# Keys' squares of a sixteen-head attention folded in half on GpSimd before VectorE sums them

## The chip, the cores and the metric

The kernel runs on one core of a Trainium2 chip. The metric is the time of one execution on the device in microseconds, the median of the runs shown. Engines are called by their names here, and in the profile's rows PE is TensorE (PEld its weight loads), DVE is VectorE, ACT is ScalarE, POOL is GpSimd and SP is SyncE.

## What is computed

A state-space block with conditioning, then six layers of local attention and a gated feed-forward net, over 128 sequences of 32 tokens and 128 channels. The change is in the attention: queries and keys of each of 16 heads (64 elements each) are divided by their norms. Since a window is 32 tokens long and a sequence too, each sequence attends to itself alone.

```python
def l2norm(t):
    return t / jnp.maximum(jnp.linalg.norm(t, axis=-1, keepdims=True), 1e-12)
...
qkv = x @ Wqkv
q, k, v = jnp.split(qkv, 3, -1)
...
q = l2norm(q) * qs
k = l2norm(k) * ksc
...
q = q * cos * scale + rotate_half(q) * sin * scale
k = k * cos * inv + rotate_half(k) * sin * inv
out = local_attention(q, k, v)      # softmax(8 q k^T, masked) v
...
for i in range(DEPTH):              # 6 layers
    x = attn_layer(shift_tokens(x), ...) + x
    x = ffn_layer(shift_tokens(x), ...) + x
```

## The kernel before

The first part (`cond_block`) is the state-space block; the second (`stack`) is the six layers, and the change is there. The 4096 tokens are 32 tiles of 128 tokens (four sequences each); four tiles are a group, so a layer has 8 groups and the six layers have 48 groups and 192 tiles. The residual stream stays in SBUF.

Every engine runs its own hand-written list, `body(i, l, g)`: for each group the same steps in the same order, with a loop over the tiles j = 0 to 3 inside. The work is pipelined over tiles by the order of those lists: a step written with `back` works on the tile (or group) that many places earlier. While the projections of tile n run, the scores of tile n - 2 are scaled and exponentiated and the values of tile n - 3 are weighed. Engines wait for each other with semaphores that count tiles. In each layer the first two groups are written out, and the other six are a hardware loop. Two more bodies at the end drain the pipeline.

For tile n the norm work goes like this. TensorE projects the queries into a PSUM tile `pa` (L843). ScalarE squares them into `sq`, an area of SBUF of 128 x 1024 floats (`square_q`, L1041). VectorE sums each head's 64 squares (`sum_squares`, L1278, called with c = 0) into `ss`, and multiplies the queries by the cosine table (L1285) and the sine table (L1294). The same area `sq` then takes the squares of the keys (`square_k`, L1048), which wait for `sum_q`; `sq_k` tells that they are there. VectorE multiplies the keys by sine and cosine and then sums their squares (`sum_squares` with c = 1), which sets `sum_k`. ScalarE turns the sums into inverse norms `inv` (L1065, L1072, L1080). The next `square_q` waits for `sum_k`, since it writes over `sq`.

GpSimd's list for a tile, before: `norm_scores` of tile n - 2 (L1470, `sm` times the queries' inverse norm, after VectorE has subtracted the maximum, L1316), `rotate` of the queries and of the keys of tile n (L1454 twice), `norm_probs` of tile n - 2 (L1492, after `rden`), `norm_keys` of tile n (L1463). Every second tile it also makes the rounding remainder `xs_lo` (L1440), in tile 2 of a group the remainder of a piece of the next layer's weights (L1485), and in the second group of a layer those of `wo` (L1479, 128 x 1024) and `w1` (L1475, 128 x 682) and the next rotary tables.

VectorE's list for a tile, before: maximum of the scores (L1309), `turn_probs` of tile n - 3 (L1303, writes `prT` after `norm_probs`), sum of the queries' squares, queries times cosine and sine, `subtract_maximum` (L1316), keys times sine and cosine, sum of the keys' squares, denominators (L1323) and their reciprocals, `oT_lo` (L1354). In tile 0 it also has the normalisation (L1342) and `fn_lo` (L1348, `fx` minus `fn_hi`, all three in SBUF) of an earlier group's feed-forward net; TensorE needs `fn_lo` for that net's first gate block (L960), which stands in its list in tile 1. In tile 3 it adds the attention to the residual (L1364).

TensorE's `project_v` of tile n waits for `sin_q` and `cos_q` of that tile, because it writes the PSUM tile that the queries leave. Its transposes (L872) wait for `oT_lo` of an earlier tile or for `norm_k`.

## Time and profile before

| | |
|---|---|
| median of 3 runs | 2878.83 us |
| lowest, highest | 2873.51, 2882.35 us |
| span of the profiled execution | 2876.3 us |
| mean granted TensorE clock | 0.988 of full speed |
| second part, from the first `fn_lo` to the last | 503.1 to 2856.6 us |
| busy: TensorE matmul, weight loads | 2709.0, 2060.1 us |
| busy: VectorE, ScalarE, GpSimd | 2616.4, 2273.1, 2115.9 us |

The rows below are from this one profiled execution. A busy share is an average over the whole span. A row of a timeline gives the start from the beginning of the span, then how long the instruction is recorded; consecutive instructions of an engine overlap by some hundredths of a microsecond in the record. What stands in brackets at a row's end is how long the engine sat idle before the instruction and which instruction's end released it. A row that groups instructions gives their number, the time that they are busy in total, the mean of one in nanoseconds, and the idle time ahead of them.

### The profile page before, as it was taken

The page shows a single profiled execution, that of the slowest core. Times are in us where ns is not written, and L with a number is a line of the kernel's source. Part 1 is how long each engine was busy: PE and PEld are TensorE (multiplying, and loading weights), DVE is VectorE, ACT ScalarE, POOL GpSimd, SP SyncE. Part 2 cuts the span into 40 slices and gives each one's busy share as a digit, 9 for nine tenths or more (in the row PEclk, how much of TensorE's full clock was granted, in tenths as well). Part 3 has the DMA queues.
Part 4 walks back from the last instruction along what each step waited for, and adds up shares of the span by engine and source line. Part 5 has one row for each costly group of instructions (what it writes and reads, how often), then busy time and mean ns, then how long its engine had stood idle before and what let it go on. Part 6 is the DMA issues. An engine that isn't in the chain of part 4 may idle for free.

```text
span 2876.3 us, 92923 instructions
## 1 busy us (share of the span) xinstructions
PE 2709.0 (94%) x36417; PEld 2060.1 (72%) x36417; DVE 2616.4 (91%) x3375; ACT 2273.1 (79%) x3824; POOL 2115.9 (74%) x1529
## 2 busy tenths in 40 slices
PE   8799978999999999999999999999999999999996
PEld 7577756777777777777777777777777777777774
DVE  6899968999999999999999999999999999999993
ACT  5799857878787887878788887878888787877873
POOL 5766658777778777777777787777777777877771
PEclk9899999999999999999999999999999999999998
DMA  1000013222223232232232233222322322322222
GB/s 57 23 2 2 1 36 76 70 71 65 71 63 76 71 76 64 66 78 67 67 76 68 66 74 73 69 67 68 75 68 66 78 65 63 72 67 58 63 66 78
DMA packets 103719, 178.41 MB, mean 62 GB/s; under 512 B 29350, under 2 KB 52708, under 8 KB 103396
## 3 DMA queue, kind: packets, MB, share of 16 engines
q1 hardware_dynamic: 102372, 174.60, 25.0%
q8 instruction: 124, 2.03, 0.3%
q10 hardware_dynamic: 1152, 1.20, 0.1%
q14 instruction: 71, 0.58, 0.1%
HBM read 22.62 MB, written 2.10 MB: 9 GB/s over the span
## 4 chain that ended last, share of the span: by engine, by line
POOL 26%; issue 24%; DVE 15%; PE 11%; ACT 5%; DMA 2%; POOLq 0%; DVEq 0%; SPq 0%; ACTq 0%
POOL spare L1454 15%; DVE spare L1285 5%; POOL pr L1492 4%; DVE qk_t L1294 3%; POOL spare L1463 3%; PE pa L843 3%; DVE ss L1278 3%; PE px L872 3%; DMA kT<-spare 2%; POOL xs_lo L1440 2%; DVE oT_lo L1354 1%; PE pg L982 1%; PE pg L930 1%; PE px L917 1%; POOL w_lo L1485 1%
## 5 line engine op out<-in xcount | busy, mean ns | idle before, releaser
L1454 POOL TENSOR_TENSOR spare<-spare,qk_t 128x1024 f32<-128x1024 f32 x384 | 910.2, 2393 | 11.5 <-POOL xs_lo L1440 8.1
L843 PE MATMUL pa<-w_hi,xs_hi 128*128 128x512 f32 x1152 | 511.8, 444 | 27.5 <-issue 8.4
L1470 POOL TENSOR_TENSOR sm<-sm,inv 128x512 f32<-128x512 f32 x192 | 201.8, 1051 | 446.7 <-DVE sm L1316 372.7
L1294 DVE TENSOR_TENSOR qk_t<-pa,rot 128x1024 f32<-128x1024 f32 x384 | 464.4, 1210 | 1.9 <-ACT spare L1048 1.7
L1285 DVE TENSOR_TENSOR spare<-pa,rot 128x1024 f32<-128x1024 f32 x384 | 464.5, 1210 | 0.0
L1278 DVE TENSOR_REDUCE ss<-spare 128x16 f32<-128x1024 f32 x384 | 457.5, 1191 | 6.7 <-ACT spare L1041 5.9
L843 PE MATMUL pa<-w_hi,xs_lo 128*128 128x512 f32 x1152 | 456.7, 396 | 0.0
L843 PE MATMUL pa<-w_lo,xs_hi 128*128 128x512 f32 x1152 | 454.9, 395 | 0.0
L872 PE MATMUL px<-ident_sb,spare 128*128 128x128 f32 x3072 | 409.0, 276 | 22.3 <-POOL spare L1463 11.6
L1463 POOL TENSOR_TENSOR spare<-spare,inv 128x1024 f32<-128x1024 f32 x192 | 365.9, 1906 | 80.6 <-ACT inv L1080 75.7
L872 PEld LDWEIGHTS px<-ident_sb,spare 128*128 128x128 f32 x3072 | 341.6, 141 | 111.0 <-issue 59.0
L843 PEld LDWEIGHTS pa<-w_hi,xs_hi 128*128 128x128 f32 x1152 | 217.9, 189 | 120.9 <-DVE qk_t L1294 45.5
L1354 DVE TENSOR_TENSOR oT_lo<-px,oT_hi 128x1024 fp32r<-128x1024 f32 x192 | 226.5, 1180 | 83.3 <-ACT oT_hi L1118 83.3
L903 PEld LDWEIGHTS ps<-kT,qT 128*32 128x32 f32 x12288 | 181.8, 110 | 128.7 <-issue 64.7
L903 PE MATMUL ps<-kT,qT 128*32 128x64 f32 x12288 | 212.2, 221 | 56.0 <-DMA kT<-spare 55.9
L1095 ACT COPY spare<-px 128x1024 f32<-128x1024 f32 x192 | 194.6, 1013 | 87.9 <-PE px L872 87.6
L1048 ACT ACTIVATE spare<-pa 128x1024 f32<-128x1024 f32 x192 | 196.5, 1024 | 77.3 <-DVE ss L1278 59.7
L843 PEld LDWEIGHTS pa<-w_hi,xs_lo 128*128 128x128 f32 x1152 | 217.7, 189 | 53.6 <-issue 0.5
L843 PEld LDWEIGHTS pa<-w_lo,xs_hi 128*128 128x128 f32 x1152 | 218.9, 190 | 49.1 <-issue 12.3
L1118 ACT CAST oT_hi<-px 128x1024 fp32r<-128x1024 f32 x192 | 193.4, 1007 | 69.5 <-PE px L917 68.1
L917 PEld LDWEIGHTS px<-pT,spare 64*64 64x64 f32 x12288 | 198.9, 136 | 68.9 <-issue 66.0
L241 PE MATMUL c_bank<-c_h,c_cdiag 64*64 64x256 f32 x2048 | 230.3, 380 | 10.4 <-DVE c_h L548 9.1
(180 smaller groups left out, 5970.0 us busy)
## 6 DMA issues: line engine op xcount, KB each, us to landing
kT<-spare SPq DMA_DIRECT2D x384, 256.0 KB, 3.7
pT<-prT SPq DMA_DIRECT2D x768, 64.0 KB, 2.0
w_part<-in_Wqkv SPq DMA_DIRECT2D x40, 192.0 KB, 3.7
wo<-in_Wo SPq DMA_DIRECT2D x6, 512.0 KB, 5.4
c_h<-in_x SPq DMA_DIRECT2D x4, 512.0 KB, 9.0
spare<-in_x SPq DMA_DIRECT2D x8, 256.0 KB, 5.0
out<-spare SPq DMA_DIRECT2D x8, 256.0 KB, 2.5
wo<-in_W SPq DMA_DIRECT2D x6, 341.0 KB, 5.2
```

The source lines that it names most:

```text
L241: last = pe.matmul(py[t % 2][rows, 0:DI], cdiag[rows, t % 3, n, :], h[rows, t % 2, n, :], start=False, stop=(n == DS - 1), skip_group_chec ...
L843: last = pe.matmul(pa[(u + c) % 2][:, half * 512:half * 512 + 512], x[:, j * P:(j + 1) * P], w[:, at], start=(k == 0), stop=(k == 2))
L872: last = pe.transpose(px[:, hp * P:(hp + 1) * P], qk_r[:, c, hp * P:(hp + 1) * P], ident[:])
L903: last = pe.matmul(ps[rows, hp * 2 * S:(hp + 1) * 2 * S], qT[:, hp, rows], kT[:, :, hp, b, :], start=False, stop=True, skip_group_check=True)
L917: last = pe.matmul(px[at:at + DH, to:to + 64], v[rows, j, h * DH:(h + 1) * DH], pT[rows, :, h, :], start=True, stop=True, skip_group_check ...
L1278: dve.reduce_sum(ss[:, c, :], heads(sq), AX.X).then_inc(s[sum_sem], 1)
L1285: dve.tensor_tensor(heads(qk_r[:, c, :]), heads(pa[(3 * j + c) % 2][:]), per_head(rot[:, l % 2, 2 * c, :]), ALU.mult).then_inc(s[cos], 1)
L1294: dve.tensor_tensor(halves(qk_t[:, c, :]), halves(pa[(3 * j + c) % 2][:])[:, :, ::-1, :], table.unsqueeze(1).to_broadcast([P, HEADS, 2, DH ...
L1354: dve.tensor_tensor(oT_lo[:, :, k, :].rearrange("p h (r q) -> p r h q", r=2), px[:].rearrange("p (r h q) -> p r h q", r=2, h=HP), oT_hi[:, ...
L1454: pool.tensor_tensor(qk_r[:, c, :], qk_r[:, c, :], qk_t[:, c, :], ALU.add)\
L1463: pool.tensor_tensor(k_r, k_r, over(inv[:, j % 2, 1, :], DH), ALU.mult).then_inc(s["norm_k"], 1)
L1470: pool.tensor_tensor(keys(sm[:]), keys(sm[:]), over(inv[:, j % 2, 0, :], S), ALU.mult)\
```

## The change

The sum of the keys' squares is made in two steps. GpSimd first adds, for each head, the upper 32 of the 64 squares to the lower 32, in place in `sq` (`fold_squares_k`), and signals `folded_k`. VectorE then sums the lower 32 of each head alone, behind `folded_k` in place of `sq_k`. The queries' squares are summed as before. The fold is the first step of GpSimd's list for every tile.

```diff
--- before.py
+++ after.py
@@ -664,7 +664,7 @@
 
         names = """const_loaded mask_ready zeroed xs_zeroed w_part_loaded w0_hi w0_ready wo_loaded kT_ready ffn_loaded
             qk_scale_loaded rot_ready w_hi_ready w_lo_ready xs_hi_ready xs_ready q_full k_full v_full
-            sq_q sq_k sum_q sum_k floored ln_done inv_ready
+            sq_q sq_k sum_q folded_k sum_k floored ln_done inv_ready
             cos_q cos_k sin_q sin_k rot_q rot_k norm_k tq_done tq_out tk_done tk_out v_out
             masked scores_done top_done sub_done scaled exp_done den_done rden_done probs_done turned pT_loaded pv_done pv_out oT_lo_ready wo_hi_ready wo_lo_ready
             wo_done res_attn fs_ready center_done fc_ready fsq_ready var_done fln_done frs_ready fn_mul fn_ready fn_hi_ready fn_lo_ready w1_loaded w1_hi_ready w1_lo_ready
@@ -1270,12 +1270,19 @@
 
             @block.vector
             def _(dve):
-                def sum_squares(i, j, back, c, sq_sem, sum_sem):
-                    n, j, live = tile(i, j, back)
-                    if live:
-                        dve.wait_ge(s[sq_sem], n + 1)
+                def sum_squares_q(i, j, back):
+                    n, j, live = tile(i, j, back)
+                    if live:
+                        dve.wait_ge(s["sq_q"], n + 1)
                         wait_for(dve, s["floored"], n)
-                        dve.reduce_sum(ss[:, c, :], heads(sq), AX.X).then_inc(s[sum_sem], 1)
+                        dve.reduce_sum(ss[:, 0, :], heads(sq), AX.X).then_inc(s["sum_q"], 1)
+
+                def sum_squares_k(i, j, back):
+                    n, j, live = tile(i, j, back)
+                    if live:
+                        dve.wait_ge(s["folded_k"], n + 1)
+                        wait_for(dve, s["floored"], n)
+                        dve.reduce_sum(ss[:, 1, :], heads(sq)[:, :, 0:DH // 2], AX.X).then_inc(s["sum_k"], 1)
 
                 def times_cos(i, j, l, c, sq_sem, transposed, cos):
                     n, j, live = tile(i, j, 0)
@@ -1388,7 +1395,7 @@
                             add_ffn(i, 2)
                         maximum(i, j, 2)
                         turn_probs(i, j, 3)
-                        sum_squares(i, j, 0, 0, "sq_q", "sum_q")
+                        sum_squares_q(i, j, 0)
                         if j == 2:
                             gated(i, 2, 2)
                         times_cos(i, j, l, 0, "sq_q", "tq_done", "cos_q")
@@ -1396,7 +1403,7 @@
                         subtract_maximum(i, j, 2)
                         times_sin(i, j, l, 1, "sq_k", "rot_k", "sin_k")
                         times_cos(i, j, l, 1, "sq_k", "tk_done", "cos_k")
-                        sum_squares(i, j, 0, 1, "sq_k", "sum_k")
+                        sum_squares_k(i, j, 0)
                         if j == 3:
                             add_attention(i, 1)
                         if j == 0:
@@ -1454,6 +1461,13 @@
                         pool.tensor_tensor(qk_r[:, c, :], qk_r[:, c, :], qk_t[:, c, :], ALU.add)\
                             .then_inc(s[rotated], 1)
 
+                def fold_squares_k(i, j, back):
+                    n, j, live = tile(i, j, back)
+                    if live:
+                        pool.wait_ge(s["sq_k"], n + 1)
+                        low, high = heads(sq)[:, :, 0:DH // 2], heads(sq)[:, :, DH // 2:DH]
+                        pool.tensor_tensor(low, low, high, ALU.add).then_inc(s["folded_k"], 1)
+
                 def norm_keys(i, j, back):
                     n, j, live = tile(i, j, back)
                     if live:
@@ -1513,6 +1527,7 @@
 
                 def body(i, l, g):
                     for j in range(GT):
+                        fold_squares_k(i, j, 0)
                         norm_scores(i, j, 2)
                         if j == 3:
                             shift_lo(i, -1, 0)
```

GpSimd's list from the last step of tile 3 of a group to tile 0 of the next group (here the first and second group of layer 0). L1463 is `norm_keys`, L1470 `norm_scores`, L1454 `rotate` of queries and keys, L1492 `norm_probs`. Before:

```order
L1463 TENSOR_TENSOR spare<-spare,inv 128x1024 [waits inv_ready,rot_k]
L1470 TENSOR_TENSOR sm<-sm,inv 128x512 [waits inv_ready,sub_done]
L1454 TENSOR_TENSOR spare<-spare,qk_t 128x1024 [waits cos_q,sin_q]
L1454 TENSOR_TENSOR spare<-spare,qk_t 128x1024 [waits cos_k,sin_k]
L1492 TENSOR_TENSOR pr<-pr,rden 128x512 [waits rden_done]
L1463 TENSOR_TENSOR spare<-spare,inv 128x1024 [waits inv_ready,rot_k]
```

And now, the same piece of the list (the line numbers are those of the changed kernel; L1477 is `norm_keys`, L1469 the fold, L1484 `norm_scores`, L1461 `rotate`, L1506 `norm_probs`):

```order
L1477 TENSOR_TENSOR spare<-spare,inv 128x1024 [waits inv_ready,rot_k]
L1469 TENSOR_TENSOR spare<-spare 128x16x32 [waits sq_k]
L1484 TENSOR_TENSOR sm<-sm,inv 128x512 [waits inv_ready,sub_done]
L1461 TENSOR_TENSOR spare<-spare,qk_t 128x1024 [waits cos_q,sin_q]
L1461 TENSOR_TENSOR spare<-spare,qk_t 128x1024 [waits cos_k,sin_k]
L1506 TENSOR_TENSOR pr<-pr,rden 128x512 [waits rden_done]
L1477 TENSOR_TENSOR spare<-spare,inv 128x1024 [waits inv_ready,rot_k]
```

The fold stands between the keys' norms of one tile and the scaling of the scores in the next, with a wait on `sq_k`; all else keeps its order.

VectorE's list around the sum of the keys' squares, tile 3 of a group. L1316 is `subtract_maximum`, L1294 and L1285 are the keys times sine and cosine, L1278 is the sum, L1364 adds the attention. Before:

```order
L1316 TENSOR_TENSOR sm<-ps,top 128x512 [waits exp_done,top_done]
L1294 TENSOR_TENSOR qk_t<-pa,rot 128x1024 [waits rot_k,sq_k]
L1285 TENSOR_TENSOR spare<-pa,rot 128x1024 [waits tk_done,sq_k]
L1278 TENSOR_REDUCE ss<-spare 128x16 [waits floored,sq_k]
L1364 TENSOR_TENSOR res<-pg,res 128x512 [waits wo_done]
```

And now (L1323, L1301, L1292, L1285 and L1371 in the changed kernel):

```order
L1323 TENSOR_TENSOR sm<-ps,top 128x512 [waits exp_done,top_done]
L1301 TENSOR_TENSOR qk_t<-pa,rot 128x1024 [waits rot_k,sq_k]
L1292 TENSOR_TENSOR spare<-pa,rot 128x1024 [waits tk_done,sq_k]
L1285 TENSOR_REDUCE ss<-spare 128x16 [waits floored,folded_k]
L1371 TENSOR_TENSOR res<-pg,res 128x512 [waits wo_done]
```

Nothing moved on VectorE; the sum waits for `folded_k` where it waited for `sq_k`, and its input is half as long.

## Rows read from the trace of the kernel before

**Rows 1.** The page, busy time of each engine (share of the span, instructions).

```profile
PE 2709.0 (94%) x36417; PEld 2060.1 (72%) x36417; DVE 2616.4 (91%) x3375; ACT 2273.1 (79%) x3824; POOL 2115.9 (74%) x1529
```

**Rows 2.** Groups of instructions: busy us, mean ns | idle before (L1475: min/median/max ns).

```profile
L1454 POOL TENSOR_TENSOR spare<-spare,qk_t 128x1024 f32<-128x1024 f32 x384 | 910.2, 2393 | 11.5 <-POOL xs_lo L1440 8.1
L1470 POOL TENSOR_TENSOR sm<-sm,inv 128x512 f32<-128x512 f32 x192 | 201.8, 1051 | 446.7 <-DVE sm L1316 372.7
L1278 DVE TENSOR_REDUCE ss<-spare 128x16 f32<-128x1024 f32 x384 | 457.5, 1191 | 6.7 <-ACT spare L1041 5.9
...
L1323 DVE TENSOR_REDUCE den<-pr 128x16 f32<-128x512 f32 x32 | 21.6, 674 | 0.0
L1485 POOL TENSOR_TENSOR w_lo<-w_part,w_hi 128x384 f32 x6 | 6.1, 1018 | 0.0
...
L1475 POOL TENSOR_TENSOR w_lo<-wo,w_hi x6: 1682/1686/1689, 494.5 to 2506.3; 128x682 fp32r<-128x682 f32 x6
```

**Rows 3.** Timeline of ScalarE, tile 3, then tiles 0 and 1 of the next group.

```profile
1436.76 1.03 ACT L1048 ACTIVATE spare<-pa 128x1024 f32<-128x1024 f32 x1 [1.35 <-DVE ss L1278]
...
1451.40 1.02 ACT L1048 ACTIVATE spare<-pa 128x1024 f32<-128x1024 f32 x1
...
1454.99 0.62 ACT L1110 ACTIVATE pr<-sm 128x512 f32<-128x512 f32 x1
...
1459.89 0.31 ACT L1080 ACTIVATE inv<-ln_ss,norm_c 128x32 f32<-128x32 f32 x1
...
1463.97 1.02 ACT L1048 ACTIVATE spare<-pa 128x1024 f32<-128x1024 f32 x1
```

**Rows 4.** All `fn_lo` (L1348): min/median/max ns, starts; who waited for it (us, times).

```profile
L1348 DVE TENSOR_TENSOR fn_lo<-fx,fn_hi x48: 691/1134/1211, 503.1 to 2856.6; 128x512 fp32r<-128x512 f32 x48
...
  PEld pg L960: 18.3, 36
```

**Rows 5.** Timeline of GpSimd over the same tiles.

```profile
1439.51 1.05 POOL L1470 TENSOR_TENSOR sm<-sm,inv 128x512 f32<-128x512 f32 x1 [1.99 <-DVE sm L1316]
...
1452.94 1.05 POOL L1470 TENSOR_TENSOR sm<-sm,inv 128x512 f32<-128x512 f32 x1 [2.44 <-DVE sm L1316]
1453.95 4.73 POOL L1454 TENSOR_TENSOR spare<-spare,qk_t 128x1024 f32<-128x1024 f32 x2
1458.64 1.05 POOL L1492 TENSOR_TENSOR pr<-pr,rden 128x512 f32<-128x512 f32 x1
1460.35 1.91 POOL L1463 TENSOR_TENSOR spare<-spare,inv 128x1024 f32<-128x1024 f32 x1 [0.66 <-ACT inv L1080]
...
1465.56 1.05 POOL L1470 TENSOR_TENSOR sm<-sm,inv 128x512 f32<-128x512 f32 x1 [1.72 <-issue]
```

**Rows 6.** Timeline of VectorE, tiles 0 and 1 of that group.

```profile
1452.18 0.68 DVE L1316 TENSOR_TENSOR sm<-ps,top 128x512 f32<-128x512 f32 x1
...
1455.04 1.21 DVE L1278 TENSOR_REDUCE ss<-spare 128x16 f32<-128x1024 f32 x1
...
1459.11 1.13 DVE L1348 TENSOR_TENSOR fn_lo<-fx,fn_hi 128x512 fp32r<-128x512 f32 x1 [0.30 <-ACT fn_hi L1194]
...
1460.76 0.70 DVE L1303 STREAM_TRANSPOSE prT<-pr 128x512 f32<-128x512 f32 x1
```

**Rows 7.** TensorE: timeline in tile 1; waits over the span (us, times, longest).

```profile
1464.88 0.19 PEld L843 LDWEIGHTS pa<-w_hi,xs_hi 128*128 128x128 f32 x1 [0.29 <-DVE qk_t L1294]
...
PE px L872 <- DVE oT_lo L1354: 7.1, 35, 0.4
```

**Rows 8.** Timelines of GpSimd and VectorE at the start of the second part.

```profile
391.18 1.31 POOL L1440 TENSOR_TENSOR xs_lo<-res,xs_hi 64x256 fp32r<-64x256 f32 x1 [0.36 <-ACT xs_hi L684]
392.57 1.50 POOL L1440 TENSOR_TENSOR xs_lo<-res,xs_hi 64x248 fp32r<-64x248 f32 x1
...
392.14 1.44 DVE L1424 TENSOR_TENSOR w_lo<-spare,w_hi 128x1024 fp32r<-128x1024 f32 x1 [0.23 <-ACT w_hi L1266]
393.50 1.66 DVE L1424 TENSOR_TENSOR w_lo<-spare,w_hi 128x1024 fp32r<-128x1024 f32 x1
```

## Prediction, made before the changed kernel ran

> **What bounds the kernel now.** I read the page first: GpSimd is the least busy of the four (2115.9 us), VectorE is busy for 2616.4 us, 91% of the span, and TensorE's matmuls for more still [rows 1]. Busy shares can't tell which of them sets the pace, so next come the timelines of one group of four tiles, engine by engine. The groups are alike: 48 instructions that write `fn_lo`, one per group, start between 503.1 and 2856.6 us [rows 4], which is 50.07 us per group. I call the tiles of a group 0 to 3.
>
> In tile 0 the chain is this. ScalarE squares the keys from 1451.40 to 1452.42 [rows 3]. VectorE's subtraction (L1316) ends at 1452.86 [rows 6], and GpSimd, idle 2.44 us until then, scales the scores at 1452.94, rotates queries and keys until 1458.68, and normalises the probabilities (L1492) until 1459.69 [rows 5]. VectorE issues `fn_lo` (L1348) at 1459.11, released by ScalarE's `fn_hi`, and it ends at 1460.24 [rows 6]: 1.13 us, for an instruction whose shortest took 0.69 us [rows 4]. In 46 of the 48 groups it ends 0.54 to 0.56 us after L1492 of GpSimd does, wherever it began; the two others, in the last two groups, ran in 0.69 us with GpSimd's work done or about to be. So `fn_lo`, the only instruction of VectorE in these groups that reads two tensors from SBUF, waits until GpSimd's instruction lets go. TensorE waits for it in 36 groups [rows 4], with the first gate block.
>
> Behind `fn_lo`, VectorE takes the maximum and turns the probabilities at 1460.76 (which needs L1492), sums the squares of the next queries, and multiplies by cosine and sine [rows 6]. The sine product releases TensorE: the first weights of the value projection of tile 1 load at 1464.88, after 0.29 us of waiting for just that [rows 7]. From there to the next group's centring TensorE's matmuls follow one another nearly without a gap; its waits for `oT_lo` come to 7.1 us in the whole kernel [rows 7]. So one thread runs GpSimd, VectorE, TensorE, ScalarE and back, and a GpSimd instruction in tile 0 stands on it; most of VectorE's time in tiles 1 to 3 doesn't.
>
> **The change, part by part.** VectorE's sum over the keys' squares goes from 128x1024 to 128x512. The old one is 1.191 us [rows 2], the same reduction over 512 elements (L1323) 0.674 us [rows 2]: 0.517 us less, 192 times, 99 us of VectorE's time. The wait on `folded_k` behind which that sum now stands costs nothing in itself: in tile 0 the sum had its turn at 1455.04 [rows 6], and the fold, by what follows, ends near 1453.85. Behind the sum in VectorE's queue stand the denominators and `oT_lo`; they come earlier, not later.
>
> GpSimd gains 192 adds of 512 elements, two tensor inputs. No row is that size. Its neighbours with two full inputs are 384 columns at 1.018 us, 682 at 1.686 [rows 2] and 1024 at 2.393 [rows 2]; the line through the first and the last gives 1.018 + 128 x 2.148 ns = 1.29 us, which I take. The ends are 1.05 us (L1470, 512 columns with one input broadcast) and 1.69. At 1.29 it adds 248 us to GpSimd's 2116, 82% of the span, so GpSimd doesn't become the bound by its load.
>
> What counts is the fold's place in GpSimd's queue. It waits for `sq_k` of the newest tile and stands ahead of the scaling of the scores, the two rotations, the probabilities and the keys' norms. In tile 3 it fits in GpSimd's idle time, 1.99 us: the squares end at 1437.79 [rows 3], 1.72 us before the scaling starts at 1439.51 [rows 5]; tile 2 has more room (some 2.2 us). In tile 0: squares end 1452.42, a signal from ScalarE takes some 0.14 us (`inv` ends at 1460.20 [rows 3], GpSimd starts on it at 1460.35 [rows 5]), fold 1.29, so scaling starts near 1453.81 (instructions overlap by 0.04) and not at 1452.94: 0.87 us late. In tile 1 the squares end at 1464.99 [rows 3], fold to 1466.42, scaling near 1466.38 and not 1465.56 [rows 5]: 0.8 us late. Nothing takes that from tile 1 to TensorE: VectorE then turns the probabilities of tile 2 some 0.6 us late, still ahead of what TensorE needs, and the shorter sum gives the time back before the attention is added. ScalarE's exponential in tile 0 began at 1454.99 [rows 3] and its input would now be there at 1454.9: just covered.
>
> In tile 0 the delay stands on the thread. Rotation of the keys now ends at 1458.68 + 0.87 = 1459.55. VectorE, whose 0.5 us from the shorter sum end as a longer wait for `fn_hi`, issues `fn_lo` at 1459.11 still, so it now meets the rotation, and L1492 is queued right behind. Who gets the memory at 1459.55? The start of this part of the kernel has the mirror of it [rows 8]: GpSimd's instruction ends at 392.49, VectorE's, issued 392.14, ends 1.09 us later, and GpSimd's next, issued 392.57, ends at 394.07, 0.49 us behind it; VectorE's next was issued at 393.50, ahead of VectorE's own end at 393.58, and yet ends 1.09 us after GpSimd's 394.07. The two take turns. By that `fn_lo` ends at 1459.55 + 0.55 = 1460.10, 0.14 us earlier than before, but L1492 only then runs, 0.91 to 1.05 us, to 1461.0 or 1461.15. The turning of the probabilities slips from 1460.76 to 1461.08 or 1461.22, and with it, instruction by instruction, the sine product and the value projection: 0.32 to 0.46 us per group. 46 groups at 0.39 are 18 us. Given back are at most the 7.1 us that TensorE waits for `oT_lo` [rows 7], since that follows the shorter sum. The second group of each layer has 2.4 us of weights' remainder on GpSimd ahead of the scaling in tile 1, where nothing hides the fold: 6 times 0.3, 2 us. Sum: +18 - 7 + 2 = +13 us.
>
> The profiled execution's span is 2876.3 us and the median 2878.83; I take the difference, 2.5 us, as what lies around it, and add to the median: 2892.
>
> The Trainium skill ("SBUF — State Buffer", section "SBUF: two separate sides") says that a VectorE instruction with two SBUF inputs and a GpSimd instruction that reads SBUF hold their shared ports as an exclusive lock, so that "the other fully blocks". The rows agree as to the wait. The page doesn't say who is next when both wait, which is what separates 2892 from the rival below.
>
> **Rivals.** *GpSimd keeps the memory.* If its queued L1492 starts before `fn_lo` gets in (it is recorded as starting 0.04 us before the rotation ends [rows 5]), `fn_lo` ends 0.55 us after 1460.56, at 1461.11, 0.87 us later than now, and so does the first gate block: 46 x 0.87 = 40, less 7: +33, 2912 us. For it: GpSimd's instructions overlap, with no gap to slip in. Against it: [rows 8].
>
> *Not slower: the fold is hidden.* In tile 0 the slip of the turning is the fold's price less 0.90 to 1.04 us. At the cheap end, 1.05 us, it is 0.01 to 0.15 us, and the kernel keeps what it is given back: between 2878.8 - 7 = 2872 and 2879. It decides below about 1.1 us. For it: L1470 handles 512 columns in 1.05 us. Against it: that row reads 16 values as its second input, the fold reads 512. It also holds if another thread, ScalarE's unbroken work in tile 0, sets the pace where I see GpSimd's.
>
> *VectorE is the bound by its load.* Then all 99 us come off: 2779 us. For it: 2616 of 2876 us busy, and hardly any idle time in tiles 1 and 2. Against it: TensorE has none there either. The Trainium skill ("Perfetto Trace Analysis", section "Identifying the Most-Contended Engine") would have it by the occupancy of VectorE, with TensorE judged by its weight loads (72% here [rows 1]); the trace speaks against it, with TensorE's matmuls back to back in the very stretch where VectorE is full.
>
> **How the numbers follow.** Taking turns (2892, by the ends of 0.32 and 0.46 us and of the returned waits 2886 to 2902, with a fold of 1.69 us some 15 more): 0.45. GpSimd keeps the memory (2912): 0.25. Hidden (2872 to 2879): 0.24. VectorE's load: 0.03. Something else: 0.03. About 0.3%, 8.6 us, is what a measurement of this kernel can tell from no change. Slower by more than that: 0.36 of the first, the second, and 0.01: 0.62. Within it: 0.09 of the first, 0.21 of the third, 0.01: 0.31. Faster: 0.07. The range, 2869 to 2917, takes in the first three cases except the top of the second.
>
> **What would show it.** The fold (L1469) near 1.29 us, 192 times; GpSimd's scaling of the scores in tile 0 released by `sq_k` and the fold and not by VectorE's subtraction; `fn_lo` no longer ending 0.55 us behind the probabilities but behind the keys' rotation, and L1492 longer than 1.05 us in that tile; VectorE waiting longer before `prT`, and TensorE before the value projection of tile 1. VectorE busy down to about 2517 us with its idle time up by more. I am wrong if the fold is at 1.1 us or less, if `fn_lo` ends behind L1492 still, or if TensorE's waits shrink by tens of microseconds.

## The result, and the profile after

| | before | after |
|---|---|---|
| median | 2877.26 us (6 runs) | 2893.84 us (6 runs, 2889.11 to 2896.05) |
| ratio, 95% interval | | 1.0052, 1.004 to 1.0064 |
| span of the profiled execution | 2876.3 us | 2893.8 us |
| VectorE busy | 2616.4 us | 2530.3 us |
| GpSimd busy | 2115.9 us | 2376.4 us |
| first `fn_lo` to last | 503.1 to 2856.6 us | 503.9 to 2873.8 us |

VectorE was relieved of 86 us and the kernel takes 16.6 us more. The answers to [rows 1] and [rows 2] are these lines of the page after: the busy times, and the costliest groups with their busy time, the mean ns of one, and the idle time before them.

```profile
PE 2726.6 (94%) x36416; PEld 2052.7 (71%) x36417; DVE 2530.3 (87%) x3375; ACT 2277.1 (79%) x3824; POOL 2376.4 (82%) x1721
...
L1469 POOL TENSOR_TENSOR spare<-spare 128x512 f32<-128x512 f32 x192 | 246.6, 1284 | 195.6 <-ACT spare L1048 195.5
...
L1484 POOL TENSOR_TENSOR sm<-sm,inv 128x512 f32<-128x512 f32 x192 | 202.1, 1053 | 70.2 <-DVE sm L1323 70.1
```

The fold (L1469) takes 1.284 us, where 1.29 was interpolated. The lines have moved: `norm_scores` is L1484, `rotate` L1461, `norm_probs` L1506, `norm_keys` L1477, `fn_lo` L1355, the turning of the probabilities L1310.

Tile 0 of the group that answers to [rows 5] and [rows 6], first GpSimd's timeline, then VectorE's (start, duration, engine, line, and in brackets the idle time before it with what ended it):

```profile
1457.70 1.29 POOL L1469 TENSOR_TENSOR spare<-spare 128x512 f32<-128x512 f32 x1 [2.23 <-ACT spare L1048]
1458.96 1.05 POOL L1484 TENSOR_TENSOR sm<-sm,inv 128x512 f32<-128x512 f32 x1
1459.97 4.73 POOL L1461 TENSOR_TENSOR spare<-spare,qk_t 128x1024 f32<-128x1024 f32 x2
1464.66 1.50 POOL L1506 TENSOR_TENSOR pr<-pr,rden 128x512 f32<-128x512 f32 x1
```

```profile
1464.31 0.94 DVE L1355 TENSOR_TENSOR fn_lo<-fx,fn_hi 128x512 fp32r<-128x512 f32 x1 [0.67 <-ACT fn_hi L1194]
...
1466.29 0.71 DVE L1310 STREAM_TRANSPOSE prT<-pr 128x512 f32<-128x512 f32 x1 [0.44 <-POOL pr L1506]
```

The scaling of the scores now follows the fold and not the subtraction. `fn_lo` is issued while the keys' rotation runs, ends at 1465.25, 0.55 us behind the rotation's end at 1464.70, and then the probabilities take 1.50 us and not 1.05, ending at 1466.16, 0.91 us behind `fn_lo`. In 46 of the 48 groups `fn_lo` ends 0.54 to 0.56 us behind the rotation. VectorE then waits for the probabilities. The whole span's waits (us in total, times, longest) show the same; these are of after:

```profile
POOL spare L1469 <- ACT spare L1048: 195.5, 175, 2.8
...
DVE prT L1310 <- POOL pr L1506: 77.1, 145, 2.3
PEld pa L843 <- DVE qk_t L1301: 74.4, 143, 3.7
PEld px L872 <- POOL spare L1477: 57.9, 107, 2.6
```

And these of before:

```profile
PEld pa L843 <- DVE qk_t L1294: 45.5, 115, 3.8
PEld px L872 <- POOL spare L1463: 32.1, 51, 2.5
DVE prT L1303 <- POOL pr L1492: 20.8, 52, 2.0
```

That TensorE waits longer for the sine product (`qk_t`) and VectorE for the probabilities (`pr`) was foreseen. The third wasn't: TensorE's transposes of the keys (L872) wait for `norm_keys` (L1477) in 107 places and not in 51. The 51 of before lie nearly all in tile 3 of a group, and none in tile 1 of a regular group; of the 107 some 45 are in tile 1, where in the regular groups the transposes begin 0.05 us behind the end of `norm_keys`. (About as many are in tile 0, but there they begin 0.4 us behind that end, so that something else, which I haven't found, lets them go.) What the wait in tile 1 costs is the second half of the price in the regular groups.

**Where the 16.4 us between first and last `fn_lo` come from.** The interval from one `fn_lo` to the next tells stretches of the kernel apart. I numbered the intervals 1 to 8 from the first one on, over and over, so that the same number is the same place of a layer:

| intervals | before, mean | after, mean | together |
|---|---|---|---|
| 2 to 5 of every layer (24) | 50.13 us | 50.34 us | +5.2 us |
| 1 of every layer (6) | 50.77 | 50.56 | -1.2 |
| 6 and 7 of layers 1 to 5 (10) | 50.38 | 50.52 | +1.4 |
| 8 of layers 1 to 5 (5) | 50.67 | 51.81 | +5.7 |
| the last two of all | 44.35 | 47.05 | +5.4 |

Only a third comes from the groups that I had worked out. The eighth intervals have the weights' remainder `wo_lo` on GpSimd, right ahead of the fold of tile 1. GpSimd after, and then before, at the same place of the same layer:

```profile
1671.52 2.41 POOL L1493 TENSOR_TENSOR wo_lo<-wo,wo_hi 128x1024 fp32r<-128x1024 f32 x1
1673.88 1.28 POOL L1469 TENSOR_TENSOR spare<-spare 128x512 f32<-128x512 f32 x1
1675.13 1.04 POOL L1484 TENSOR_TENSOR sm<-sm,inv 128x512 f32<-128x512 f32 x1
```

```profile
1664.55 2.41 POOL L1479 TENSOR_TENSOR wo_lo<-wo,wo_hi 128x1024 fp32r<-128x1024 f32 x1
1666.92 1.05 POOL L1470 TENSOR_TENSOR sm<-sm,inv 128x512 f32<-128x512 f32 x1
```

Scaling is 1.25 us later behind the remainder, and VectorE meets it. The first row is VectorE after, the second before:

```profile
1681.92 0.71 DVE L1310 STREAM_TRANSPOSE prT<-pr 128x512 f32<-128x512 f32 x1 [1.67 <-POOL pr L1506]
```

```profile
1674.32 0.70 DVE L1303 STREAM_TRANSPOSE prT<-pr 128x512 f32<-128x512 f32 x1
```

The last two intervals are the thin end of the pipeline, where no new tile comes in and no fold runs. The stretch between the last two `fn_lo`, after and then before (length, busy time and instructions of PE, PEld, DVE, ACT and POOL, granted clock, DMA share, GB/s):

```profile
2828.00:2873.84 45.84, 33.66 (x256) 20.42 (x248) 11.73 (x17) 12.18 (x17) 2.10 (x2) 0.64 0.26 69
```

```profile
2816.82:2856.60 39.78, 26.08 (x239) 16.09 (x231) 11.73 (x18) 12.18 (x17) 2.09 (x2) 0.84 0.29 80
```

VectorE, ScalarE and GpSimd do the same work in the same time; TensorE is busy for 7.6 us more at a mean granted clock of 0.64 against 0.84. That is a longer stay at the lower level of 1.2 GHz, and the fold has no instruction there. The experiments below fall into the same two classes in this stretch (0.64 to 0.69, with the last two intervals together 92.3 to 94.1 us; or 0.83 to 0.84, with 87.1 to 89.1 us) and not by what they fold, so some 5 us of a difference of two spans can be this alone. The stretch itself is kept only for the profiled execution of each kernel. Of the others the time and the mean granted clock are known: in the executions beside the experiments the kernel before took 2876.3 us on average in the 20 of its executions at 0.988 and 2882.5 us in the 4 at 0.985, and the changed kernel 2889.11 us in the one at 0.988 and 2895.1 us in the two at 0.985. So one kernel moves by some 6 us with its clock, and at equal clock (0.988, 0.987, 0.985) the two kernels are 12.9, 14.3 and 12.5 us apart, less than the 16.6 us of the medians. Because of it I read the experiments by two numbers: the ratio, and the regular groups.

**How the tables below are made.** Mean way from the subtraction of the maximum (L1316 before) of one tile to that of the next, in the regular intervals (2 to 5) between 1075 and 2780 us, 16 or 17 groups for each kernel, worked out from the starts in the timelines of VectorE. "Late" is how long GpSimd's scaling starts after the subtraction has ended, beyond the usual 0.08 us in tile 0 and 0.14 us in tile 1.

| | 0 to 1 | 1 to 2 | 2 to 3 | 3 to 0 | sum | late in tile 0 | late in tile 1 |
|---|---|---|---|---|---|---|---|
| before | 12.57 | 12.49 | 11.64 | 13.45 | 50.13 | 0 | 0 |
| after | 12.74 | 12.67 | 11.65 | 13.31 | 50.36 | 0.66 | 0.29 |

So a regular group of the changed kernel loses 0.17 us in tile 0 and 0.18 us in tile 1, and gets 0.14 us back at its end. In the eighth intervals, behind the remainder, the same ways are 12.96 and 14.38 us, and before 12.60 and 13.31: 0.36 and 1.07 us longer.

### The profile page after: what moved, and what is told of

It reads as the page before. It is cut to its first block, busy times and chain, and to the rows that moved or that the text cites. A ratio compares the mean times of both kernels' runs of the same rounds, so it can differ in the third digit from the quotient of the medians.

```text
span 2893.8 us, 93120 instructions
## 1 busy us (share of the span) xinstructions
PE 2726.6 (94%) x36416; PEld 2052.7 (71%) x36417; DVE 2530.3 (87%) x3375; ACT 2277.1 (79%) x3824; POOL 2376.4 (82%) x1721
## 4 chain that ended last, share of the span: by engine, by line
PE 40%; issue 17%; POOL 17%; DVE 6%; ACT 3%; DMA 2%; POOLq 0%; ACTq 0%; DVEq 0%; SPq 0%
PE pa L843 13%; PE pg L930 8%; POOL spare L1461 8%; PE px L872 5%; PE px L917 4%; PE pg L982 4%; PE ps L903 3%; PE pg L974 2%; POOL spare L1477 2%; POOL pr L1506 2%; POOL sm L1484 2%; DVE spare L1292 2%; DVE qk_t L1301 2%; DVE ss L1278 2%; DMA kT<-spare 2%
## 5 line engine op out<-in xcount | busy, mean ns | idle before, releaser
L1461 POOL TENSOR_TENSOR spare<-spare,qk_t 128x1024 f32<-128x1024 f32 x384 | 911.3, 2396 | 3.8
L1292 DVE TENSOR_TENSOR spare<-pa,rot 128x1024 f32<-128x1024 f32 x384 | 464.8, 1210 | 0.0
L1301 DVE TENSOR_TENSOR qk_t<-pa,rot 128x1024 f32<-128x1024 f32 x384 | 464.7, 1211 | 0.0
L872 PE MATMUL px<-ident_sb,spare 128*128 128x128 f32 x3072 | 411.4, 277 | 21.6 <-POOL spare L1477 19.0
L872 PEld LDWEIGHTS px<-ident_sb,spare 128*128 128x128 f32 x3072 | 337.5, 141 | 117.3 <-POOL spare L1477 57.9
L1469 POOL TENSOR_TENSOR spare<-spare 128x512 f32<-128x512 f32 x192 | 246.6, 1284 | 195.6 <-ACT spare L1048 195.5
L1477 POOL TENSOR_TENSOR spare<-spare,inv 128x1024 f32<-128x1024 f32 x192 | 366.6, 1909 | 22.8 <-ACT inv L1080 22.5
L1484 POOL TENSOR_TENSOR sm<-sm,inv 128x512 f32<-128x512 f32 x192 | 202.1, 1053 | 70.2 <-DVE sm L1323 70.1
```

The lines of the kernel that those rows point to most:

```text
L872: last = pe.transpose(px[:, hp * P:(hp + 1) * P], qk_r[:, c, hp * P:(hp + 1) * P], ident[:])
L1292: dve.tensor_tensor(heads(qk_r[:, c, :]), heads(pa[(3 * j + c) % 2][:]), per_head(rot[:, l % 2, 2 * c, :]), ALU.mult).then_inc(s[cos], 1)
L1301: dve.tensor_tensor(halves(qk_t[:, c, :]), halves(pa[(3 * j + c) % 2][:])[:, :, ::-1, :], table.unsqueeze(1).to_broadcast([P, HEADS, 2, DH ...
L1461: pool.tensor_tensor(qk_r[:, c, :], qk_r[:, c, :], qk_t[:, c, :], ALU.add)\
L1469: pool.tensor_tensor(low, low, high, ALU.add).then_inc(s["folded_k"], 1)
L1477: pool.tensor_tensor(k_r, k_r, over(inv[:, j % 2, 1, :], DH), ALU.mult).then_inc(s["norm_k"], 1)
```

## The experiments

Every kernel here computes what the reference does; those with an idle add do that add besides. `FOLDED` is the set of tiles of a group whose keys are folded; the others sum all 64 squares as before. The results of the regular groups are collected at the end of this section.

**Tile 0 left out.** The change in tiles 1 to 3 alone.

```diff
+FOLDED = (1, 2, 3)
 def fold_squares_k(i, j, back):
-    if live:
+    if live and j in FOLDED:
 def sum_squares_k(i, j, back):
-    dve.wait_ge(s["folded_k"], n + 1)
-    dve.reduce_sum(ss[:, 1, :], heads(sq)[:, :, 0:DH // 2], AX.X)
+    (the same for j in FOLDED; else wait for sq_k and sum all of heads(sq))
```

> The fold is made in tiles 1, 2 and 3 of a group only; in tile 0 VectorE sums all 64 squares per head, as before. My theory (the price sits in tile 0 alone: the fold pushes GpSimd's probabilities behind fn_lo): the slip of 0.39 us per group is gone and the small gain from the shorter sums stays, 2870 to 2879 us, and in the trace fn_lo ends 0.55 us behind the probabilities (L1506) again. Rival (a fold costs wherever it stands in GpSimd's queue, about 16.6 us / 4 per tile): 2889 us. Rival (VectorE's load is the bound): 2877 less 3/4 of 99 us, 2803 us.

Measured: 2900.89 us, ratio 1.0095 (1.008 to 1.0111). I expected a gain, and it is slower than the whole change. My account, with the thread through tile 0 only, can't be all. The way from tile 1 to tile 2 has grown by 0.66 us. Its trace says who waits. GpSimd's `norm_keys`, then TensorE's transposes of those keys:

```profile
1431.50 1.90 POOL L1482 TENSOR_TENSOR spare<-spare,inv 128x1024 f32<-128x1024 f32 x1
```

```profile
1433.46 0.86 PEld L873 LDWEIGHTS px<-ident_sb,spare 128*128 128x128 f32 x8 [0.73 <-POOL spare L1482]
```

The same two of before:

```profile
1422.32 1.91 POOL L1463 TENSOR_TENSOR spare<-spare,inv 128x1024 f32<-128x1024 f32 x1
```

```profile
1424.28 0.96 PEld L872 LDWEIGHTS px<-ident_sb,spare 128*128 128x128 f32 x8
```

In the folded kernel the transposes begin 0.06 us behind the end of `norm_keys` (1433.40), after 0.73 us of idle time. Before, they began 0.05 us behind it too (1424.23 and 1424.28), and no wait is listed. But it is one: in all 24 regular groups of before the distance is 0.053 to 0.054 us, and where TensorE plainly waits (this run, tile 1 alone, the whole change) it is 0.051 to 0.053. The 0.05 us are what the signal takes, and TensorE stood idle ahead of them for 0.05 to 0.10 us, too short for the list of waits. A spare time looks otherwise: with tile 0 alone folded (next run) the transposes of tile 1 begin 0.14 to 0.20 us behind `norm_keys`. So before the change TensorE had nothing to spare there, and the fold of tile 1 stands ahead of that `norm_keys` in GpSimd's list: `norm_keys` ends 9.53 us behind the tile's subtraction in this run and 8.92 us before, in the mean of the regular groups.

**Tile 0 alone.** The same edit with `FOLDED = (0,)`.

> The fold is made in tile 0 of a group only; in tiles 1 to 3 VectorE sums all 64 squares per head, as before. My theory: the whole price is there, 46 x 0.32 to 0.46 us, and almost nothing is given back, since the shorter sum of tile 0 ends in the wait for fn_hi: 2891 to 2898 us. Rival (a fold costs wherever it stands): 2881 us.

Measured: 2892.87 us, ratio 1.006 (1.0046 to 1.0074), as expected. The way from tile 0 to tile 1 grows by 0.31 us, at the lower end of the 0.32 to 0.46, and it alone.

**Tile 1 alone**, to see whether tile 1's path is what made the first run slow. `FOLDED = (1,)`.

> The fold is made in tile 1 of a group only. Theory (tile 1 is the second costly place: its late norm_keys holds TensorE's transposes of the keys in tile 2): the way from tile 1's subtraction to tile 2's grows by 0.57 us as in e1, the rest stays: 46 x 0.57 = 26 us, ratio 1.008 to 1.010 against the kernel before. As tile 0's fold alone costs 0.6%, the two prices then overlap in the changed kernel (0.52% together). Rival (tile 1's price comes only together with folds in tiles 2 and 3): ratio below 1.003.

Measured: 2907.25 us, ratio 1.0109 (1.0094 to 1.0124), a little above the expected range. One tile's fold costs twice what all four do. The way from tile 1 to tile 2 is 0.62 us longer with scaling 0.76 us late: all but some 0.14 us of the delay arrives.

**Tiles 2 and 3 alone**, where the fold fits in GpSimd's idle time. `FOLDED = (2, 3)`.

> The fold is made in tiles 2 and 3 of a group only. What the first runs showed (with folds in tiles 1 to 3 the way from tile 1's subtraction to tile 2's grew by 0.57 us, the one from tile 3's to the next tile 0's shrank by 0.13) makes tile 1 a second costly place: GpSimd's norm_keys ends late there and TensorE's transposes of the keys wait for it. Theory now: tiles 2 and 3 cost nothing and give 0.13 us per group, 46 x 0.13 = 6 us less than before, 2866 to 2873 us. Rival (each fold costs by its load on GpSimd): 2883 us or more.

Measured: 2875.12 us against 2878.57, ratio 0.9986 (0.9977 to 0.9995). The return exists, in the way from tile 3 to tile 0 (-0.14 us), and is 6 us by 46 groups, 4 us by the ratio. (The expected range, 2866 to 2873 us, was for a kernel before at 2875 us; by the ratio the gain is a little smaller than was expected.)

**The read that takes turns, removed.** `fn_lo` is made to read a PSUM tile, so that it has only one input in SBUF; once in the changed kernel, once in the kernel before.

```diff
 def scale_shift(i, back):
-    act.activation(fx[:], fx[:], ACT.Identity, ...)
+    act.activation(pg[:], fx[:], ACT.Identity, ...)
 def round_normed(i, back):
-    act.copy(fn_hi[:], fx[:])
+    act.copy(fn_hi[:], pg[:])
...
-    dve.tensor_tensor(fn_lo[:], fx[:], fn_hi[:].bitcast(F32), ALU.subtract)
+    dve.tensor_tensor(fn_lo[:], pg[:], fn_hi[:].bitcast(F32), ALU.subtract)
```

> The changed kernel, with one difference in the feed-forward net: ScalarE writes the scaled normalised values into the PSUM tile pg (free at that time) and not into fx in SBUF, so that VectorE's fn_lo (pg minus fn_hi) reads one tensor from SBUF. My theory (what costs is the place that fn_lo takes ahead of the probabilities): fn_lo takes 0.69 us wherever GpSimd is, the probabilities take 1.05 us and end 0.87 us later than in the kernel before, at which time VectorE has come to prT anyway; no slip against the kernel before, some of its wait for fn_lo saved: 2864 to 2875 us. Rival (GpSimd's 0.87 us delay costs by itself, without the turn that fn_lo takes): 2885 us or more.

> The kernel before, with fn_lo reading pg from PSUM as in e3 and no fold. My theory: fn_lo ends at its issue + 0.69 us, 0.44 us earlier than now, and TensorE's first gate block and VectorE's prT move up by 0.3 to 0.44 us per group: 46 x 0.35 = 16 us less, 2856 to 2866 us. Rival (fn_lo's wait is covered by TensorE's or ScalarE's own work): 2874 to 2880 us.

Measured: the changed kernel 2891.86 us, ratio 1.0059 (1.0045 to 1.0073) to before; the kernel before with the edit 2863.29 us, ratio 0.9962 (0.9948 to 0.9975). The second was expected, the first was a miss. The instruction itself does what was thought in both; group of `fn_lo` in the changed kernel with the edit, then in the kernel before with it (ns shortest/median/longest), and after without it:

```profile
L1355 DVE TENSOR_TENSOR fn_lo<-pg,fn_hi x48: 690/691/693, 502.9 to 2866.5; 128x512 fp32r<-128x512 f32 x48
```

```profile
L1348 DVE TENSOR_TENSOR fn_lo<-pg,fn_hi x48: 690/692/692, 502.7 to 2846.7; 128x512 fp32r<-128x512 f32 x48
```

```profile
L1355 DVE TENSOR_TENSOR fn_lo<-fx,fn_hi x48: 693/937/961, 503.9 to 2873.8; 128x512 fp32r<-128x512 f32 x48
```

So the 0.44 us by which the median in [rows 4] exceeds the shortest is the two engines' shared read: with one input elsewhere `fn_lo` takes 0.69 us every time. (The edit also shortens ScalarE's two instructions on these values, from 0.825 to 0.797 and from 0.617 to 0.579 us, so a small part of the gain can be that.) The Trainium skill ("SBUF — State Buffer", section "SBUF: two separate sides") has the pair block each other; the traces agree, and the run adds that `fn_lo` from PSUM isn't blocked. The changed kernel is no faster by the ratio since tile 1 takes over: its tile 0 gains 0.46 us, but in tile 1 the scaling is 0.71 us late and not 0.29, and the way from there is 13.08 us and not 12.67. The kernel before with the read from PSUM gains 0.50 us in tile 0 and loses 0.16 in tile 1, where the transposes stand 0.05 us behind `norm_keys` in every regular group as well.

**Tile 0's fold, without the turns.** `FOLDED = (0,)` with the read from PSUM.

> The fold is made in tile 0 only, and fn_lo reads pg from PSUM as in e4. If the price of tile 0's fold is the turn that fn_lo takes ahead of the probabilities, it is nearly gone without the shared memory read: the way from tile 0's subtraction to tile 1's grows by 0.14 us against e4 (12.10 to 12.24, as in e3), 46 x 0.14 = 6 us above e4: 2865 to 2872 us. If GpSimd's delay of 0.87 us costs by itself: the same 17.7 us as in e2, 2879 to 2883 us.

Measured: 2874.96 us, ratio 0.9992 (0.9983 to 1.0001), so 0.30% above the kernel before with that read, where with both inputs in SBUF tile 0's fold cost 0.60%. The time lies between the two that I had put up. But in tile 0 itself the price is the same (+0.36 us here, +0.31 us there). Half of it is taken back in the way from tile 1 to 2 (12.49 us against 12.65), where the kernel without the fold was held up already: `norm_keys` ends 9.25 us behind the subtraction there, and 8.90 us with the fold in tile 0. So the theory of the turns, by which the way in tile 0 was to grow by 0.14 us, is wrong: the price in tile 0 needs no turns.

**Tiles 2 and 3 with the read from PSUM**, the two edits that gained.

> As e9, and fn_lo reads pg from PSUM as in e3 and e4. Theory: the two gains add, since one is in tile 0 and one in tiles 2 and 3: 2863 - 6, 2853 to 2861 us. Rival (they are the same slack of TensorE): 2862 to 2866 us.

Measured: 2864.88 us against 2878.57, ratio 0.9957 (0.9944 to 0.9971). The gains hardly add, as the rival had it: the way from tile 3 to tile 0 is 13.43 us again, where the changed kernel with the same read has 13.30. Why the return vanishes here I haven't found.

**An idle add of GpSimd, at the fold's place in tile 0**, in the kernel before: a delay alone, with VectorE's sum untouched. Two sizes, W = 256 and W = 512; `pad` is a tile of its own.

```diff
+def idle_add(i, j):
+    n, j, live = tile(i, j, 0)
+    if live and j == 0:
+        pool.wait_ge(s["sq_k"], n + 1)
+        pool.tensor_tensor(pad[:, 0:W], pad[:, 0:W], pad[:, 0:W], ALU.add)
...
 for j in range(GT):
+    idle_add(i, j)
     norm_scores(i, j, 2)
```

> The kernel before, with one GpSimd addition of 128x256 on a tile of its own that nobody reads, in tile 0 at the fold's place and behind the same wait on sq_k (0.73 us by an instruction of that length; VectorE's sums are as before). If the two engines take turns at instruction ends: the keys' rotation then ends at 1458.99, before fn_lo is issued (1459.11), so fn_lo stands behind the probabilities, which end 0.31 us late, and everything moves by 0.31 us: 46 x 0.31 = 14 us, 2886 to 2892 us, nearly as much as the whole fold in tile 0. If what counts is only how far GpSimd's addition exceeds the cover that tile 0 has (0.9 to 1.0 us): 2873 to 2878 us. If the price goes by length: 17.7 x 0.73 / 1.29 = 10 us, 2885 us.

> The kernel before, with one GpSimd addition of 128x512 on a tile of its own in tile 0, behind sq_k, nobody waiting for its result; VectorE's sums are as before. Theory (the shorter sum of tile 0 brings nothing, since VectorE waits there for fn_hi anyway): the same price as e2, ratio 1.005 to 1.007. Rival (the shorter sum gives back its 0.52 us): ratio 1.012 or more.

Measured: W = 256 2882.98 us, ratio 1.0014 (1.0005 to 1.0023); W = 512 2879.82 us, ratio 1.0011 (1.0001 to 1.0021). Both below what I expected, for one reason: the adds were shorter than I had put them. The groups of `pad`, W = 256, then W = 512:

```profile
L1462 POOL TENSOR_TENSOR pad<-pad x48: 612/613/617, 400.3 to 2763.2; 128x256 f32<-128x256 f32 x48
```

```profile
L1462 POOL TENSOR_TENSOR pad<-pad x48: 1038/1040/1042, 400.2 to 2762.7; 128x512 f32<-128x512 f32 x48
```

By what they did deliver the pair says more than was hoped. The short one makes scaling 0.11 us late and costs 0.10 us per group; the long one makes it 0.56 us late and costs 0.08 us. The two ratios alone can't be told apart; the regular groups can. In the first `fn_lo` is still behind the probabilities, in the second it has got in ahead of them. Their groups of `fn_lo`, W = 256, then W = 512:

```profile
L1349 DVE TENSOR_TENSOR fn_lo<-fx,fn_hi x48: 692/1250/1271, 502.8 to 2862.3; 128x512 fp32r<-128x512 f32 x48
```

```profile
L1349 DVE TENSOR_TENSOR fn_lo<-fx,fn_hi x48: 691/693/1605, 502.0 to 2861.6; 128x512 fp32r<-128x512 f32 x48
```

**Tile 0's fold, started earlier**, so that it would end before the subtraction does: `FOLDED = (0,)`, and ScalarE squares the keys before it rounds the shifted states.

```diff
 copy_qT(i, j, 1)
-if j == 0:
-    shift_hi(i, 0, 1)
...
 square_k(i, j, 0)
+if j == 0:
+    shift_hi(i, 0, 1)
 copy_kT(i, j, 1)
```

> As e2 (fold in tile 0 only), with ScalarE's two shift_hi copies of tile 0 (0.84 us) made behind the squares of the keys instead of ahead of them, so that sq_k comes 0.84 us earlier. Theory (the fold costs because its input comes late on ScalarE, 0.44 us ahead of the subtraction's end, while the fold takes 1.29): the fold ends at about the time at which the subtraction ends, GpSimd scales the scores at most 0.1 us later than in the kernel before, fn_lo ends behind the probabilities again, and the price of e2 (0.60%) is gone: ratio 0.999 to 1.001. Rival (GpSimd's added work costs whenever it is done): ratio 1.004 or more.

Measured: 2890.62 us, ratio 1.0048 (1.0033 to 1.0064). I expected nothing. Was it the edit on ScalarE? The control is the kernel before with that edit alone.

> The kernel before with one edit, on ScalarE alone: in tile 0 the rounding of the states' shift (L1230/L1231) stands behind the squares of the keys and not ahead of them. It is the control for the run that folded tile 0 with the same edit and took 1.0048 of the time of before, where a fold that ended in time should have cost nothing. If the edit itself costs that time (everything of ScalarE's that stands behind the squares in tile 0, down to the rounding of the state that fn_lo waits for, comes later), this kernel is at 1.003 to 1.005 of before, the way from tile 0's subtraction to tile 1's near 12.7 to 12.8 us instead of 12.56, and the fold alone near nothing there. If the edit is free and the fold costs the time in spite of its early end, this kernel is at 0.999 to 1.001.

Measured: 2877.96 us against 2877.15, ratio 1.0004 (0.9995 to 1.0013). The edit is free; the fold costs it. GpSimd and VectorE in tile 0 of the early fold:

```profile
1404.21 1.28 POOL L1474 TENSOR_TENSOR spare<-spare 128x512 f32<-128x512 f32 x1 [1.46 <-ACT spare L1049]
1405.43 1.06 POOL L1489 TENSOR_TENSOR sm<-sm,inv 128x512 f32<-128x512 f32 x1
1406.44 4.73 POOL L1466 TENSOR_TENSOR spare<-spare,qk_t 128x1024 f32<-128x1024 f32 x2
1411.12 1.06 POOL L1511 TENSOR_TENSOR pr<-pr,rden 128x512 f32<-128x512 f32 x1
```

```profile
1404.44 0.68 DVE L1328 TENSOR_TENSOR sm<-ps,top 128x512 f32<-128x512 f32 x1
...
1411.64 1.08 DVE L1360 TENSOR_TENSOR fn_lo<-fx,fn_hi 128x512 fp32r<-128x512 f32 x1 [1.12 <-ACT fn_hi L1195]
```

The subtraction ends at 1405.12, and scaling starts at 1405.43: the squares had come 0.5 us earlier and not early enough, the fold still ends some 0.3 us too late. The way from tile 0 to 1 is 12.82 us, 0.26 above the control's 12.56 with a scaling 0.26 us late. Nothing of that small delay is forgiven, because `fn_lo` here is blocked by the probabilities once more, as before, ending 0.55 us behind them.

**The regular groups of all of them.** First tile 0, from the least to the most delayed, each against its own base (the control for the early fold, the kernel with the PSUM read for the two with that read):

| | late in tile 0 | way 0 to 1, more by | `fn_lo` stands |
|---|---|---|---|
| idle add, 256 | 0.11 us | 0.10 us | behind the probabilities |
| early fold of tile 0 | 0.26 | 0.26 | behind the probabilities |
| idle add, 512 | 0.56 | 0.08 | ahead of them, but for some groups |
| after | 0.66 | 0.17 | ahead of them |
| tile 0 alone | 0.80 | 0.31 | ahead of them |
| after, PSUM read | 0.65 | 0.21 | (no turns) |
| tile 0 alone, PSUM read | 0.80 | 0.36 | (no turns) |

The price of a delay there isn't a slope but a saw: as long as `fn_lo` follows the probabilities, all of it counts; once `fn_lo` slips in ahead, 0.49 us are forgiven (0.66 - 0.17, and 0.80 - 0.31) and it begins again near nothing. The 0.49 us are the change of order: as long as `fn_lo` is behind, VectorE turns the probabilities 1.07 us after they are there, since it has `fn_lo` and the maximum to do first; with `fn_lo` ahead, 0.13 us after, but the probabilities themselves end 0.45 us later for it. With the read from PSUM nothing is blocked, VectorE turns them 0.59 us after they are there, 0.13 with the fold, and 0.44 us are forgiven: nearly the same, which is why the fold costs the same there. Between 0.26 and 0.56 us late no run was made.

Then the way from tile 1 to tile 2:

| | late in tile 1 | way 1 to 2, more by |
|---|---|---|
| tile 1 alone | 0.76 us | 0.62 us |
| tiles 1 to 3 | 0.76 | 0.66 |
| after | 0.29 | 0.18 |

That is the delay less 0.10 to 0.14 us. And there is a reason why the parts don't add (0.60% and 1.09% less 0.14% alone, 0.52% together): with tile 0 folded, the subtraction of tile 1 comes 0.89 us behind the end of the keys' squares and not 0.43 (the same 0.89 in the kernel with tile 0 alone), so tile 1's fold has 0.46 us more time in which nobody waits for it.

## Why the prediction was right, and where it wasn't

2892 was said and 2893.84 measured, by the case that was called likeliest. The turns, the fold's size and the return were right; that the number is so near is in good part luck, since one step was wrong and its error was made up by others. Step by step:

- **The fold's size**: 1.29 us taken, 1.284 measured. Right, and the ends of 1.05 and 1.69 us weren't needed. The rival "hidden" would have needed 1.1 us; the idle add of 1.04 us shows that its point was about right: 0.08 us per group left.
- **Who gets the memory**: turns, in 46 of 48 groups. Had GpSimd kept it, `fn_lo` would end 0.55 us behind the probabilities. Right. What it was worth wasn't: with the read from PSUM tile 0's fold lengthens the way there by as much.
- **VectorE's load**: it had 86 us less to do (99 were foreseen from the sum alone) and nothing came of it but 0.14 us per group from tile 3 to 0. The Trainium skill ("Perfetto Trace Analysis", section "Identifying the Most-Contended Engine") would have had VectorE's occupancy decide; the measurement is against it here.
- **The return**, -7 us: tiles 2 and 3 alone give -4 by the ratio and -6 by the regular groups. Right, and it is in the whole change too (13.31 us from tile 3 to 0 and not 13.45).
- **Tile 0**, 0.32 to 0.46 us per group, +18: measured 0.17 us, +8 by 46 groups. Over-sized by the delay. Scaling came 0.66 us late and not 0.87: the squares end 0.59 us ahead of the subtraction's end and not 0.44, which they also do in the kernel with tiles 1 to 3 folded (0.60), so it is a gift of the later tiles' folds that I had left out. What is forgiven was right: 0.49 us, where my two ends forgave 0.55 and 0.41.
- **Tile 1**, "Nothing takes that from tile 1 to TensorE": this is the step that failed. I followed the scaling of tile 1 to the turned probabilities and not down GpSimd's own list to `norm_keys`, for which TensorE's transposes were waiting already, with nothing to spare. It costs 0.18 us per group in the whole change and 0.62 alone. Nor was the delay there 0.8 us, but 0.29 in the whole change (0.76 alone), since tile 0's fold moves the subtraction. The list of waits of before, 32.1 us in 51 places, wouldn't have told: nearly all those places are in tile 3. What tells is the end of `norm_keys` beside the start of the transposes, the same 0.053 us in every regular group.
- **The second group of each layer**, +2 us: the place and the reason were right (5 times, not 6), the size not. These intervals are 1.13 us longer each, 5.7 together; less the 0.23 us that every regular group pays, the place itself costs 0.9 us each, 4.5 together. The way from tile 1 to tile 2 is 1.07 us longer there with scaling 1.45 us later.
- **The end of the kernel**: +5.4 us of the difference of spans are in the last two intervals, with TensorE's clock at a mean of 0.64 against 0.84 in the last of them, and no step of mine had them.

So the sum, +13, is near the measured +15 (by the ratio) to +17 (by the medians) because of terms that cancel: tile 0 was 10 us too high, tile 1 some 8 us and the layers' second groups some 2.5 us too low, the first groups of the layers (1.2 us shorter together) had no term, and the clock at the end adds what isn't the change's own. Without the last two intervals the trace has +11 us. The regular groups show it plainly: +0.23 us per group measured, 0.39 - 0.15 = +0.24 predicted. The 0.15 is there, as 0.14; the 0.39 is 0.17 from tile 0 and 0.18 from tile 1, which had been put at nothing. What stays open: what TensorE's clock does at the end from one execution to the next, and why the return of tile 3 is lost when `fn_lo` reads from PSUM and tile 1 isn't folded.

The edits that gain are parts that don't touch GpSimd's list in tiles 0 and 1: `fn_lo` from PSUM (ratio 0.9962), and the fold in tiles 2 and 3 with it (0.9957). Their intervals overlap.

## What to carry to other kernels

Before an instruction is put into an in-order list, go down that list past it, instruction by instruction, and ask of each who waits for it and with how much to spare, up to the end of the list's period, not only for the instruction that you have in mind. A consumer that has nothing to spare can be missing from the list of waits, as here, where its idle time was 0.05 to 0.10 us; it shows when the end of the one row is set beside the start of the other, group after group: always the same 0.05 us means that it waits, and a distance that varies and is larger (0.14 to 0.20 us in the run with tile 0 alone) means that it doesn't. And price such a delay where it lands: here the same fold costs 0.60% in one tile, 1.09% in the next, and is worth 0.14% in the two after them.

## What the hardware showed that I had not expected

- VectorE's `fn_lo`, with two inputs in SBUF, and GpSimd's instructions take turns at the ends of instructions when both want to read SBUF at once. It shows as a fixed distance: `fn_lo` ends 0.54 to 0.56 us behind whichever GpSimd instruction it met, and the next GpSimd instruction, though its record begins before `fn_lo` ends, ends 0.91 us behind `fn_lo` (recorded 1.50 us for a 1.05 us instruction). So a queued instruction's recorded time on GpSimd contains its wait. Whether the two alternate by rule or are served in the order in which they ask isn't shown: in [rows 8] and in the changed kernel the one that came next had also asked first.
- A GpSimd add of 128x512 takes 1.04 us when both inputs are the same tile (and 0.61 us at 128x256), and 1.28 us when they are two halves of each head's squares, as in the fold. The fold also reads in pieces of 32; but its 1.284 us lie on the line through the whole rows with two different inputs (1.29 us), so it is the second input that costs and hardly the pieces. By the price of the fold the idle add was not a fair stand-in.
- In the thin end of the kernel, with the same instructions on the other engines, TensorE's mean granted clock between the last two `fn_lo` is 0.64 to 0.69 in seven of the fourteen kernels' profiles and 0.83 to 0.84 in the other seven, and the last two intervals differ by some 5 us with it.
